# An edge bias added by VectorE out of PSUM instead of by a product on TensorE, and the message's two halves made on other engines

## What is computed

```
h    = relu(layernorm(x))                                # per node, 128 wide
m_e  = relu([h[src], h[dst]] @ W1[t] + b1[t]) @ W2[t] + b2[t]      # t = type of edge e
agg  = segment_sum(m_e, dst)                             # per node
r, z = sigmoid(gates of agg and h)
n    = tanh(i_n + r * (h_n + b_hn))
out  = x + (1 - z) * n + z * h
```

## Time and profile before

| | |
|---|---|
| median of 3 runs | 1748.21 us (1745.63 to 1748.54) |
| the profiled execution's own time | 1746.99 us |
| its span, first to last instruction | 1745.1 us |
| busy: PE, DVE, ACT, POOL | 1618.8, 1645.1, 1455.9, 1015.6 us |
| granted TensorE clock over the span | 1.000 |

### The profile page before, as it was taken

The page is one execution under the profiler, slowest core; times in us unless marked ns, Lnnn a source line. Parts: engine busy times, 40 slices in busy tenths (PEclk is TensorE's granted clock), DMA queues, the critical chain, the costliest instruction groups (busy, mean ns, idle before and its releaser), DMA issues.

```text
span 1745.1 us, 43079 instructions
## 1 busy us (share of the span) xinstructions
PE 1618.8 (93%) x10182; PEld 1422.8 (82%) x10182; DVE 1645.1 (94%) x4809; ACT 1455.9 (83%) x3401; POOL 1015.6 (58%) x1343
## 2 busy tenths in 40 slices
PE   0236999999999999999999999999999999999998
PEld 0225888888888888888888888888888888888887
DVE  8997999999999999999999999999999999999986
ACT  0025999999898999999999999999999999999896
POOL 5745666666666666766666555555555655565500
PEclk9999999999999999999999999999999999999999
DMA  2224777777777777777777777777777777777653
GB/s 84 68 61 137 193 203 199 202 199 201 197 203 203 198 201 198 200 199 198 199 197 202 194 199 195 198 197 200 195 202 195 199 199 195 202 192 200 191 142 100
DMA packets 477561, 319.97 MB, mean 183 GB/s; under 512 B 106541, under 2 KB 463629, under 8 KB 477454
## 3 DMA queue, kind: packets, MB, share of 16 engines
q10 hardware_dynamic: 261792, 156.12, 29.1%
q1 hardware_dynamic: 186542, 107.39, 26.2%
q0 software_dynamic: 29120, 55.33, 13.1%
HBM read 212.05 MB, written 106.98 MB: 183 GB/s over the span
## 4 chain that ended last, share of the span: by engine, by line
PE 74%; ACT 0%; issue 0%; DVE 0%; ACTq 0%; DVEq 0%
PE bank L1364 14%; PE bank L1366 13%; PE bank L1365 13%; PE bank L1444 9%; PE bank L1456 4%; PE bank L1472 4%; PE bank L1455 4%; PE bank L1482 4%; PE bank L1434 4%; PE bank L1426 4%; PE bank L1468 1%; ACT n_zc L1317 0%; ACT n_r L1274 0%; DVE n_out L1088 0%; ACT n_h L1226 0%
## 5 line engine op out<-in xcount | busy, mean ns | idle before, releaser
L593 POOL DMA_INDIRECT e_x<-in_x,rows_now x816 | 821.4, 1007 | 247.2 <-issue 239.0
L1209 ACT ACTIVATE e_h<-e_x,shift,rstd 128x128 f32<-128x128 f32 x816 | 355.4, 485 | 103.3 <-DVE shift L1071 65.1
L1226 ACT ACTIVATE n_h<-n_x,shift,rstd 128x128 f32<-128x128 f32 x784 | 385.8, 492 | 0.0
L1364 PE MATMUL bank<-n_h_hi,whh_hi 128*128 128x512 f32 x588 | 248.8, 423 | 1.7 <-ACT n_zc L1317 1.2
L1364 PE MATMUL bank<-n_a_hi,wih_hi 128*128 128x512 f32 x588 | 246.9, 420 | 1.3 <-DVE bank L1111 1.3
L1444 PE MATMUL bank<-n_sel,n_win 128*128 128x256 f32 x1568 | 235.4, 292 | 0.5 <-DVE n_sel L1099 0.5
L1366 PE MATMUL bank<-n_a_hi,wih_lo 128*128 128x512 f32 x588 | 231.9, 394 | 0.0
L1366 PE MATMUL bank<-n_h_hi,whh_lo 128*128 128x512 f32 x588 | 231.7, 394 | 0.0
L1365 PE MATMUL bank<-n_h_lo,whh_hi 128*128 128x512 f32 x588 | 231.5, 394 | 0.0
L1099 DVE TENSOR_SCALAR n_sel<-iota,n_rel 128x256 fp32r<-128x256 f32 x784 | 230.0, 356 | 0.2 <-POOL n_rel L644 0.2
L1365 PE MATMUL bank<-n_a_lo,wih_hi 128*128 128x512 f32 x588 | 229.6, 390 | 0.0
(11 more groups left out here) (179 smaller groups left out, 3842.5 us busy)
## 6 DMA issues: line engine op xcount, KB each, us to landing
n_win<-messages SPq DMA_DIRECT2D x1568, 64.2 KB
messages<-e_msg ACTq DMA_DIRECT2D x204, 257.0 KB, 3.0
n_x<-in_x ACTq DMA_DIRECT2D x195, 256.0 KB
out<-n_out ACTq DMA_DIRECT2D x195, 256.0 KB
e_x<-in_x,rows_now POOLq DMA_INDIRECT x816
rows_now<-lists SPq DMA_DIRECT2D x204, 2.0 KB
lists<-picks,list_rows POOLq DMA_INDIRECT x72
w<-in_W SPq DMA_DIRECT2D x1, 512.0 KB, 5.1
```

Of the source, the lines that this page charges most:

```text
L593: G.indirect_dma_start(e_x[:, s, 2 * end + t, :], None, x, bass.IndirectOffsetOnAxis(ap=rows_now[:, s, t, end:end + 1], axis=0)).then_inc( ...
L1209: last = A.activation(e_h[:, s % 2, k, :], e_x[:, s, k, :], ACT.Relu, scale=rstd[:, slot, col + k:col + k + 1], bias=shift[:, slot, col + ...
L1226: last = A.activation(n_h[:, s % 2, cols], n_x[:, s, cols], ACT.Relu, scale=rstd[:, slot, col + 4 + k:col + 5 + k], bias=shift[:, slot, co ...
L1364: T.matmul(o, w_hi, v_hi, start=start, stop=False, skip_group_check=onto)
```

## The change

The product of ones with `b2_rows` (L1468) is left out of TensorE's step. VectorE adds the bias instead: a new step `biased` reads the message of unit `i-9` out of PSUM, adds `b2_two` (b2 spread over all partitions, which now has a buffer of its own) and writes the f32 sum into the place of the low half. ScalarE copies that into the high half, in SBUF, in the next step. GpSimd then subtracts, in place, to make the low half; VectorE's `low_half` is gone. TensorE's W1 products wait for `e_biased` in place of `e_low`, and the store stands later in ScalarE's step.

```diff
+        b2_two = sb("b2_two", [P, TYPES * D])
...
+        e_biased = sem("e_biased")
...
+            def low_half(i, m):
+                q, s = i - 10, (m - 10) % UNROLL
+                if within(q, UNITS):
+                    pool.wait_ge(e_high, q + 1)
+                    G.tensor_tensor(e_msg[:, s, :, D:2 * D], e_msg[:, s, :, D:2 * D].bitcast(F32),
+                                    e_msg[:, s, :, 0:D].bitcast(F32), ALU.subtract).then_inc(e_low, 1)
...
                 if within(i, UNITS):
                     gather(i, m, (1,))
+                low_half(i, m)
                 if h is not None:
                     write_half(h)
...
-            def low_half(i, m):
-                q, s = i - 10, (m - 10) % UNROLL
-                if within(q, UNITS):
-                    dve.wait_ge(e_high, q + 1)
-                    V.tensor_tensor(e_msg[:, s, :, D:2 * D],
-                                    bank[BE1][:, message_part].rearrange("p (t d) -> p t d", t=2),
-                                    e_msg[:, s, :, 0:D].bitcast(F32), ALU.subtract).then_inc(e_low, 1)
...
-                in_head = isinstance(i, int) and i < LAG - 2
-                if not in_head:
-                    low_half(i, m)
...
-                if in_head:
-                    low_half(i, m)
...
                     check_inputs()
+                biased(i, m)
...
+            def biased(i, m):
+                q, s = i - 9, (m - 9) % UNROLL
+                if within(q, UNITS):
+                    dve.wait_ge(e_messaged, q + 1)
+                    first = 2 * ((m - 9) % 2)
+                    V.tensor_tensor(e_msg[:, s, :, D:2 * D].bitcast(F32),
+                                    bank[BE1][:, message_part].rearrange("p (t d) -> p t d", t=2),
+                                    b2_two[:, first * D:(first + 2) * D].rearrange("p (t d) -> p t d", t=2),
+                                    ALU.add).then_inc(e_biased, 1)
...
                 normalise_edges(i, m, (0, 1))
+                q, s = i - 10, (m - 10) % UNROLL
+                if within(q, UNITS):
+                    act.wait_ge(e_biased, q + 1)
+                    act.wait_ge(e_tagged, q + 1)
+                    A.activation(e_msg[:, s, :, 0:D], e_msg[:, s, :, D:2 * D].bitcast(F32), ACT.Copy).then_inc(e_high, 1)
...
-                store_messages(i, m)
                 normalise_edges(i, m, (2, 3))
...
                     last.then_inc(e_relued, 1)
+                store_messages(i, m)
...
-                    act.wait_ge(e_messaged, q + 1)
-                    act.wait_ge(e_tagged, q + 1)
-                    A.activation(e_msg[:, s, :, 0:D], bank[BE1][:, message_part].rearrange("p (t d) -> p t d", t=2),
-                                 ACT.Copy).then_inc(e_high, 1)
...
-                        pe.wait_ge(e_low, q)
+                        pe.wait_ge(e_biased, q)
...
-                    T.matmul(bank[BE1][:, message_part], ones_r[:], b2_rows[:, first * D:(first + 2) * D],
-                             start=True, stop=False)
-                        last = T.matmul(o, e_r[:, s, t * P:(t + 1) * P], w2[:, first + t, :], start=False, stop=t == 1)
+                        last = T.matmul(o, e_r[:, s, t * P:(t + 1) * P], w2[:, first + t, :], start=True, stop=True)
```

More of the change, by code:

```diff
@@ L235, in gnn_layer @@
         descends = borrow(n_zc[:], 0, ECOLS)
-        b2_two, b2_hi, b2_lo, b2_parts = (
-            e_msg[:].rearrange("p r t w -> p (r t w)")[:, at * TYPES * D:(at + 1) * TYPES * D] for at in range(4))
-        b2_two, b2_parts = b2_two.bitcast(F32), b2_parts.bitcast(F32)
+        b2_hi, b2_lo, b2_parts = (
+            e_msg[:].rearrange("p r t w -> p (r t w)")[:, at * TYPES * D:(at + 1) * TYPES * D] for at in range(3))
+        b2_parts = b2_parts.bitcast(F32)
         ends = n_d[:].rearrange("p r w -> p (r w)").bitcast(I32).rearrange("p (k e c) -> p k e c", k=SEGMENTS, e=2)
@@ L1319, in step @@
                 normalise_nodes(i, m, (3,))
-                q, s = i - 9, (m - 9) % UNROLL
-                if within(q, UNITS):
-                    act.wait_ge(e_messaged, q + 1)
-                    act.wait_ge(e_tagged, q + 1)
-                    A.activation(e_msg[:, s, :, 0:D], bank[BE1][:, message_part].rearrange("p (t d) -> p t d", t=2),
-                                 ACT.Copy).then_inc(e_high, 1)
             pipeline(nc, act, LAST, LOOP_END, step)
```

## The result

| | before | after |
|---|---|---|
| median of 4 runs each, in one series | 1746.92 us (1744.72 to 1748.54) | 1952.92 us (1950.18 to 1966.89) |
| ratio after to before | | 1.1196 (95%: 1.114 to 1.1252) |
| the profiled execution's own time | 1746.99 us | 1954.51 us |
| its span | 1745.1 us | 1952.7 us |

The change makes the kernel 206 us slower, four times the 53 us of the forecast, and the time lies far above the range.

A forecast was written before the change was run, and what follows sets the result against it. The prediction took two closed rounds of the same length to bound the kernel: TensorE's own, and one over ScalarE and VectorE through n_out. It summed 1746.99 us + 53 for the bias = 1800 us, other terms at nothing; range 1782 to 1832.

The forecast's parts named there:

- The second round: BHN product to z gate, n_zc, n_e, n_out and back, 7.97 us; biased ahead of n_out adds 0.27 a step.
- The product with ones: Leaving it out shortens only TensorE's own round, by 0.05 to 0.12 us a step, and not the round through n_out.
- The store "costed at nothing": ScalarE's message store goes about 4.0 us later, behind e_r; costed at nothing, with thin cover.
- The cover: Time by which windows after the later store could still come without TensorE's sums being late: 0.7 us.
- Much slower by late windows: Rival: late windows or GpSimd make n_sel and the sums late, 0.2 us a step, 39 us more, 1840; chance 0.08.
- The low half, "taken at 0.7, which GpSimd's free time hides": The subtraction on GpSimd takes 0.7 us, hidden by GpSimd's 2.65 us free in a step.
- VectorE held while GpSimd makes the low half: VectorE instructions wait while GpSimd's low half runs; the forecast counted nothing for it, chance 0.05.
- The range: 1782 to 1832 us, leaving out the faster rival, no change and most of late windows; about 0.17 left out.
- The sign of late windows: TensorE's gap would stand ahead of the sums (L1444 of before) and not of the BHN product.

The follow-up runs named there:

- e1: The kernel before with VectorE's low half put ahead of n_out instead of behind it; 1799.09 us.
- e2: The kernel before with the store of messages moved behind e_r in ScalarE's step, as in the changed kernel; 1880.33 us.
- e6: The changed kernel with every group handled one step later (LAG 19 instead of 18); 1841.16 us.
- e4: The changed kernel without GpSimd's subtraction for the low half, the store waiting for the high half instead; 1878.3 us.
- e13: The kernel before with an extra write-only GpSimd operation of 800 numbers a lane, which reads nothing from SBUF; 1822.26 us.
- e10: The kernel before with an extra write-only GpSimd operation of 288 numbers a lane, which reads nothing from SBUF; 1768.53 us.
- e8: The changed kernel with LAG 19, the bias put behind n_out and the high half behind n_r; 1801.83 us.
- e12: The changed kernel with the store of out moved behind n_r, ahead of the store of messages; 1888.02 us.
- e15: The changed kernel with the store of messages put back to its old place behind n_r; 1874.2 us.

## Why the prediction was wrong

- **The second round: right.** The bias ahead of `n_out` was costed at 0.27 us x 195 = 53 us; e1 measures 52, with the wait where it was forecast. That 0.27 was so close within 0.21 to 0.40 is in part luck: no run tests the reason given for the choice. What the term is worth inside the changed kernel, where VectorE is held as well, is not shown.
- **The product with ones: not tested.** No run leaves out that product alone; in every run without it other things make the round longer.
- **The store "costed at nothing": the step that failed.** It measures 134 us alone (e2) and 119 of the 206 (the changed kernel less e6). The cover was 3.8 - 4.0 + 0.54 + 0.39 = 0.7 us, worked out with a landing of 3.24 and 2.82 from the last window's issue to `n_rel`, as one step of before shows them. Both were taken over to the new place, and neither holds there. The store now stands behind the store of `out` in its queue; the first window follows it 0.61 us later than before and `n_rel` the windows another 0.38 (medians above). That microsecond alone uses up the cover of 0.7. "Much slower by late windows" was the right mechanism at a third of its size (39 us, 0.2 a step) and with a chance of 0.08.
- **The low half, "taken at 0.7, which GpSimd's free time hides": right in length, wrong in place.** It takes 745 ns as a mean. But it stands behind gathers and starts 3.83 us behind the high half in the step shown, and in 29 steps the store waits for it: the 69.3 us of ScalarE's wait. That delay goes into the same cover.
- **VectorE held while GpSimd makes the low half: the second step that failed.** The forecast has nothing for it. The working has it that in an ordinary step the low half runs beside VectorE instructions that it doesn't hold, `n_sel` among them, and gave a chance of 0.05 to one that it does hold; that was the author's estimate, and no row of before shows it. `n_sel` is the instruction that was held most: 421 ns after, 356 before, 784 times, so 52 of the 98 us by which VectorE's busy time grew. `n_xh`, 128x512 with two inputs in SBUF, was held too: 0.68 us before, 0.96 to 1.23 us in 26 of its 196 times after, each beside a low half that had begun first, so that its mean went from 682 to 747 ns, 13 us. The groups of after:

```profile
L1098 DVE TENSOR_SCALAR n_sel<-iota,n_rel 128x256 fp32r<-128x256 f32 x784 | 282.2, 421 | 49.5 <-POOL n_rel L646 49.2
...
L654 POOL TENSOR_TENSOR e_msg<-e_msg 128x256 fp32r<-128x256 f32 x204 | 152.0, 745 | 46.7 <-ACT e_msg L1281 43.2
...
L1116 DVE TENSOR_TENSOR n_xh<-n_h,n_x 128x512 f32<-128x512 f32 x196 | 146.4, 747 | 0.2 <-issue 0.2
```

By e4 the low half costs 75 us with the rest in place.
- **The range** treated late windows and a held VectorE as rivals that exclude each other and the forecast. They come together, and each feeds the other: held VectorE, late `n_sel`; late GpSimd, late store, late windows. By the runs a step of lead gives back 119 of the 206 us, and 87 stay for the bias's place and the low half. The sign of late windows is there, the sums wait for `n_sel`, 49.9 us, and so are the longer instructions of VectorE, `n_sel` and `n_xh`.

Open: how the 87 us divide between the second round, VectorE held beside the low half, and anything else that the low half delays.

## To carry to other kernels

A store that moves takes a new place in its queue with it: cost its landing by what stands ahead of it there (3.9 us behind the store of `out` in e2), not by the landing at the old place (3.0), and don't count a cover of some tenths of a microsecond that rests on one step of one timeline. Free time on GpSimd doesn't make an operation there free: ask what VectorE runs at that moment, which may be held until that operation ends (e13's `n_sel` of 0.95 us beside 0.81 us on GpSimd), and what queues behind GpSimd's own waits. Where several small risks feed one wait, add them up instead of giving each a small chance.

## What the runs showed of the hardware

A write-only operation on GpSimd of 814 ns that nobody waits for made the kernel 75 us slower (e13), one of 385 ns 22 us (e10): twice the length, more than three times the cost. The 257 KB message store took 3.0 us as the step's first on its queue and 3.9 behind a 256 KB store (e2), as medians. And TensorE's granted clock was 0.50 from 100 to 150 us in the profile of after, 1.00 in that of before; TensorE had been busy 14.52 of the 50 us ahead of that (15.67 before). It doesn't go with the change: seven of the seventeen profiles have it, e1 and e2 among them, and e4, e8, e12 and e15 do not. It cost little, as in that part of the head VectorE is the busy one (47.66 of 50 us): e1, with 0.50 there, starts its first `n_out` 1.5 us behind the kernel before (190.4 and 188.9).
